# Attention by token: probabilities as the stationary operand of the value products

## What is computed

```python
q = l2norm((h @ Wq.T) by heads) * q_scale      # k likewise; v plain
attn = softmax(einsum('bhid,bhjd->bhij', q, k) * DH ** -0.5)
out = einsum('bhij,bhjd->bhid', attn, v)       # (b, h, 512, 64)
x = x + ga * (out.transpose(0, 2, 1, 3).reshape(b, n, 1024) @ Wo.T + bo)
```

## Time and profile before

| | |
|---|---|
| median of three runs | 1406.56 us |
| the profiled execution: its own time | 1406.78 us |
| the profiled execution: its span | 1405.0 us |
| TensorE matmul busy over the span | 1262.1 us (90%) |
| VectorE busy | 1107.3 us (79%) |
| ScalarE busy | 952.9 us (68%) |
| GpSimd busy | 858.0 us (61%) |

### The profile page before, as it was taken

How to read it: one execution, slowest core, us unless ns; L and a number is a source line. 1 busy time by engine, 2 the same in 40 slices (tenths; PEclk the granted TensorE clock), 3 DMA queues, 4 the chain that set the end, 5 groups by cost and what they waited for, 6 DMA issues and landing times. The chain is left out here.

```text
span 1405.0 us, 31811 instructions
## 1 busy us (share of the span) xinstructions
PE 1262.1 (90%) x9674; PEld 828.6 (59%) x9674; DVE 1107.3 (79%) x1995; ACT 952.9 (68%) x2014; POOL 858.0 (61%) x1659
## 2 busy tenths in 40 slices
PE   4899999989999999999899999999994477899997
PEld 4555565656555565556566555666552355677775
DVE  3778878878878887788788788877873996788887
ACT  3677677767666776677677766777762565777776
POOL 2577666766666776666667667676754664444443
PEclk8899999999999999999999999999998699999999
DMA  5000000000000000000000000000002000535341
GB/s 131 2 2 1 2 1 2 2 4 2 1 4 2 2 2 4 2 2 2 4 1 2 3 2 2 2 1 2 2 1 75 1 0 9 131 86 104 89 89 38
DMA packets 53202, 28.60 MB, mean 20 GB/s; under 512 B 8720, under 2 KB 51224, under 8 KB 53016
## 3 DMA queue, kind: packets, MB, share of 16 engines
q1 hardware_dynamic: 51832, 25.99, 7.7%
q10 hardware_dynamic: 1184, 0.40, 0.1%
HBM read 24.16 MB, written 2.23 MB: 19 GB/s over the span
## 5 line engine op out<-in xcount | busy, mean ns | idle before, releaser
L697 ACT ACTIVATE probs<-bank,neg_max 128x512 f32<-128x512 f32 x512 | 347.5, 684 | 280.3 <-DVE neg_max L815 259.5
L815 DVE TENSOR_REDUCE neg_max<-bank 128x1 f32<-128x512 f32 x512 | 329.3, 685 | 165.4 <-PE bank L516 162.0
L556 PE MATMUL bank<-probsT,qkv 128*64 128x512 f32 x1024 | 280.7, 628 | 0.9 <-DVE oT L832 0.9
L516 PE MATMUL bank<-operands 64*128 64x512 f32 x1536 | 255.9, 439 | 0.9 <-DVE operands L810 0.5
L993 POOL TENSOR_TENSOR inv_wide<-inv_sum,consts 128x512 f32<-128x512 f32 x64 | 66.5, 1039 | 237.7 <-DVE inv_sum L826 237.7
L532 PEld LDWEIGHTS T<-ident,probs 64*128 64x128 f32 x4096 | 173.6, 142 | 40.3 <-issue 10.2
L532 PE MATMUL T<-ident,probs 64*128 64x64 f32 x4096 | 173.6, 226 | 1.5 <-issue 0.7
L486 PEld LDWEIGHTS bank<-operands,hT_h 128*128 128x128 f32 x254 | 48.2, 190 | 213.0 <-issue 209.4
L516 PEld LDWEIGHTS bank<-operands 64*128 64x128 f32 x1536 | 128.4, 190 | 63.5 <-issue 44.2
L1627 POOL TENSOR_TENSOR hid_l<-gated,hid_h 128x512 fp32r<-128x512 f32 x64 | 89.4, 1397 | 123.3 <-ACT hid_h L1544 123.3
L977 POOL TENSOR_TENSOR sq<-qkv 128x256 f32<-128x256 f32 x252 | 150.9, 615 | 11.9 <-ACT qkv L676 9.7
(11 more groups left out here) (235 smaller groups left out, 2399.7 us busy)
## 6 DMA issues: line engine op xcount, KB each, us to landing
probsT<-gate_scratch SPq DMA_DIRECT2D x64, 256.0 KB, 4.9
out<-x_all SPq DMA_DIRECT2D x8, 256.0 KB, 2.3
probsT<-in_L_ffn_fc_w SPq DMA_DIRECT2D x1, 1024.0 KB, 9.4
raw<-in_L_attn_Wq SPq DMA_DIRECT2D x1, 512.0 KB, 4.4
raw<-in_L_attn_Wk SPq DMA_DIRECT2D x1, 512.0 KB, 7.3
raw<-in_L_attn_Wv SPq DMA_DIRECT2D x1, 512.0 KB, 8.6
raw_o<-in_L_attn_Wo SPq DMA_DIRECT2D x1, 512.0 KB, 8.7
probsT<-in_L_ffn_sh_w SPq DMA_DIRECT2D x2, 256.0 KB, 2.7
```

The source lines that it names most:

```text
L516: last = nc.tensor.matmul(s_bank(hp, 2 * pair + head)[:], own[rows, q, toks], own[rows, k], start=((q, k) == (QH, KH)), stop=(q == QL))
L556: last = nc.tensor.matmul(O_BANK[rows, :], qkv[:, hp % 4, j, cols], probsT[:, hp % 2, head, j], start=(j == 0), stop=(j == NT - 1), skip_g ...
L697: nc.scalar.activation(probs[:, i % 4], s_bank(hp, i)[:], ACT.Exp, bias=neg_max[:, i:i + 1], accum_out=row_sum[:, hp % 2, i:i + 1]).then_i ...
L815: nc.vector.reduce_max(neg_max[:, i:i + 1], s_bank(hp, i)[:], AX.X, negate=True).then_inc(max_done, 1)
```

## The change

The value products are turned round: for one tile t of 128 query tokens and one head, the transposed probabilities (128 keys x 128 tokens) are stationary and the values (64 columns) move, four key blocks summed. The result has tokens on the partitions, where the inverse sums already are. Hence:

- TensorE: 32 products of 64 columns per unit for 8 of 512 columns. They stand ahead of the scores of a step instead of behind the transposes of the probabilities, and tile t needs only copy t. `inverse_rows` goes, `transpose_out` (four transposes of the normalised result, in step 1, two units later) takes its place in the shared bank.
- ScalarE: copies three of four transposed tiles; `copy_inverse` goes, `high_o` (same shape, out of the shared bank) takes its place.
- VectorE: copies one of four tiles; `normalise` moves to step 0 and multiplies with a broadcast of the inverse sums; `low_o` is new, in step 1 after the two `row_max`, and reads the shared bank; `ln_rows` uses another instruction; `split_h1` goes to GpSimd.
- GpSimd: `widen` and `split_o` go, `split_h1` comes.

```diff
-                        before, count = ((t_act, 0), (t_dve, 1), (t_act, 1), (t_dve, 2))[pair]
-                        after(pe, before, 2 * u + count)
+                        before, value = ((t_act, 3 * u), (t_dve, u + 1), (t_act, 3 * u + 1), (t_act, 3 * u + 2))[pair]
+                        after(pe, before, value)
...
+                    def transpose_out(w, *free):
+                        pe.wait_ge(o_done, w + 1)
...
+                            last = nc.tensor.transpose(XT_BANK[:, t * P:(t + 1) * P], o_tok[:, t], ident[:])
+                        last.then_inc(ot_ready, 1)
...
-                            last = nc.tensor.matmul(O_BANK[rows, :], qkv[:, hp % 4, j, cols],
-                                                    probsT[:, hp % 2, head, j], start=(j == 0), stop=(j == NT - 1),
+                            at = (2 * t + head) * DH
+                            cols = slice(2 * P + head * DH, 2 * P + (head + 1) * DH)
+                            for j in range(NT):
+                                last = nc.tensor.matmul(O_BANK[:, at:at + DH], by_pair[:, t, head, j], qkv[:, hp % 4, j, cols],
+                                                        start=(j == 0), stop=(j == NT - 1))
...
-                            if pair == 1 and earlier >= 1:
-                                inverse_rows(u - 1, side)
-                                side = (r_copied, u)
+                            if pair == 1 and earlier >= 2:
+                                transpose_out(u - 2, side)
+                                side = (ol_done, u - 1)
                             if main and pair == 2 and with_next(b, hp, 1):
                                 transpose_q(u + 1, hp + 1, side)
                             if main and pair == 3 and with_next(b, hp, 1):
                                 transpose_k(u + 1, hp + 1)
+                            if earlier >= 1:
+                                weigh_values(u - 1, hp - 1, pair)
                             if main:
                                 scores(u, hp, pair)
                             if pair < 2 and earlier >= 1:
                                 transpose_probs(u - 1, pair + 2)
                             if pair >= 2 and main:
                                 transpose_probs(u, pair - 2)
-                            if pair < 2 and earlier >= 2:
-                                weigh_values(u - 2, hp - 2, pair + 2)
-                            if pair >= 2 and earlier >= 1:
-                                weigh_values(u - 1, hp - 1, pair - 2)
...
+                    def high_o(w, hp):
+                        act.wait_ge(ot_ready, w + 1)
+                        nc.scalar.activation(oT_h[:, hp % HP], XT_BANK[:], ACT.Copy).then_inc(oh_done, 1)
...
+                    def low_o(w, hp):
+                        dve.wait_ge(oh_done, w + 1)
+                        nc.vector.tensor_tensor(oT_l[:, hp % HP], XT_BANK[:], oT_h[:, hp % HP].bitcast(F32),
+                                                ALU.subtract).then_inc(ol_done, 1)
...
                                 row_max(u, hp, 2 * pair + 1)
+                            if pair == 1 and earlier >= 2:
+                                low_o(u - 2, hp - 2)
...
-                    last = nc.vector.tensor_scalar(h_ln[:, t], tile_of(b, t), mean_var[:, t, 0:1], rstd[:, t:t + 1],
-                                                   ALU.subtract, ALU.mult)
+                    last = nc.vector.scalar_tensor_tensor(out=h_ln[:, t], in0=tile_of(b, t), scalar=mean_var[:, t, 0:1],
+                                                          in1=rstd[:, t:t + 1].to_broadcast([P, C]), op0=ALU.subtract,
+                                                          op1=ALU.mult)
```

More of the change, by code:

```diff
@@ L542, in inverse_rows, with weigh_values @@
                         for t in range(NT):
[L543 to L552, removed]
+                            last = nc.tensor.transpose(XT_BANK[:, t * P:(t + 1) * P], o_tok[:, t], ident[:])
+                        last.then_inc(ot_ready, 1)
+                    def weigh_values(w, hp, t):
+                        copied, value = ((t_dve, w + 1), (t_act, 3 * w + 1), (t_act, 3 * w + 2), (t_act, 3 * w + 3))[t]
+                        pe.wait_ge(copied, value)
+                        if t == 0:
+                            after(pe, o_done, w)
                         for head in range(2):
[L554 removed]
+                            at = (2 * t + head) * DH
                             cols = slice(2 * P + head * DH, 2 * P + (head + 1) * DH)
[L556 to L559 removed]
+                            for j in range(NT):
+                                last = nc.tensor.matmul(O_BANK[:, at:at + DH], by_pair[:, t, head, j], qkv[:, hp % 4, j, cols],
+                                                        start=(j == 0), stop=(j == NT - 1))
+                        last.then_inc(av_done, 1)
                     def project_out(b, k, *free):
@@ L662, in _ @@
                     slot(B, 0, main=False)
-                    for j in (2, 3):
-                        weigh_values(HP * B - 1, HP - 1, j)
-                    project_out(LAST, 3, (r_copied, HP * B), (y_more, 3 * LAST + 2))
+                    transpose_out(HP * B - 1, (ol_done, HP * B - 1))
+                    project_out(LAST, 3, (y_more, 3 * LAST + 2))
                     transpose_y(LAST)
@@ L744, in slot @@
                                     modulate2(b - 1)
-                            if pair == 1 and earlier >= 1:
-                                copy_inverse(u - 1, hp - 1)
+                            if pair == 1 and earlier >= 2:
+                                high_o(u - 2, hp - 2)
                             if main and pair == 2 and with_next(b, hp, 1):
@@ L753, in slot @@
                                 exponentials(u, hp, 2 * pair + 1)
-                            if pair == 1 and earlier >= 1:
-                                copy_transposed(u - 1, hp - 1, 3)
+                            if pair < 2 and earlier >= 1:
+                                copy_transposed(u - 1, hp - 1, pair + 2)
                             if pair == 3 and main:
@@ L779, in _ @@
                     slot(B, 0, main=False)
+                    high_o(HP * B - 1, HP - 1)
                     for q in range(H2_EARLY, B - 1):
@@ L838, in take_mod @@
                         last.then_inc(done, 1)
[L840 to L847, removed]
                     def add_y(b, k):
@@ L915, in slot @@
                         for pair in range(NT):
-                            if pair == 2 and earlier >= 2:
+                            if pair == 0 and earlier >= 2:
                                 normalise(u - 2, hp - 2)
@@ L927, in slot @@
                                 row_max(u, hp, 2 * pair)
+                                if pair == 0 and hp == YT_HP and not is_const(b, 0):
+                                    dve.wait_ge(x1_done, b)
                                 row_max(u, hp, 2 * pair + 1)
+                            if pair == 1 and earlier >= 2:
+                                low_o(u - 2, hp - 2)
                             if main and pair == 2 and with_next(b, hp, 1):
@@ L932, in slot @@
                                 low_k(u + 1, hp + 1)
-                            if main and pair == 0 and hp == YT_HP and not is_const(b, 0):
-                                dve.wait_ge(x1_done, b)
-                            if pair == 0 and earlier >= 1:
-                                copy_transposed(u - 1, hp - 1, 2)
                             if pair == 2 and main:
@@ L946, in _ @@
                     take_mod(mod1, (CA, SA), 0, mod1_done, (h1_done, 0))
-                    for t in range(NT):
-                        split_h1(0, t)
                     sum_squares(0)
@@ L957, in _ @@
                     normalise(HP * B - 1, HP - 1)
+                    low_o(HP * B - 1, HP - 1)
                     add_y(LAST, 3)
@@ L1014, in slot @@
                             inverse_std(pool, h1_nth(b + 1))
-                        if main and with_next(b, hp, 2):
-                            square_projection(u + 2, hp + 2, 0)
-                        if earlier >= 2:
-                            split_o(u - 2, hp - 2)
-                        if main and with_next(b, hp, 2):
-                            for t in range(1, NT):
+                        for t in range(NT):
+                            if main and with_next(b, hp, 2):
                                 square_projection(u + 2, hp + 2, t)
+                            if main and hp == HP - 3 and not is_const(b, LAST):
+                                split_h1(b + 1, t)
                     def batch(b):
@@ L1025, in batch @@
                             slot(b, hp)
+                    for t in range(NT):
+                        split_h1(0, t)
                     normalise_qk(0, 0)
```

74 lines of the change are left out of this document (27 added, 47 removed).

## The result

The changed kernel takes 1756.22 us (median of 4 runs, 1752.23 to 1759.18) for 1409.73 of the kernel before beside it: a ratio of 1.2458, 95% interval 1.2402 to 1.2513. The forecast was 1733 with a range of 1600 to 1950; the difference forecast was 327 us, measured 346.5. The profiled execution, the slowest of the four, has a span of 1757.5 us, 352.5 more than before.

What follows compares the result with a forecast made beforehand. TensorE, full in every step, bounds the kernel: plus 49.0 us a batch for products and waits, minus 7.6, gives 41.4, times 8 = 331, 327 after the edges; span 1405 + 327 = 1732, forecast 1733 us, range 1600 to 1950.

Steps and rivals of the forecast that it cites:

- What bounds the kernel: Attention stretch: TensorE has no room, busy 967 of 1020 us, so a microsecond more in a step lengthens the whole.
- The products: Value products on TensorE: loads 0.111 us apart, 1.77 us a step for 1.01, plus 3.08 a unit.
- third rival: Value products: loads not hidden, load and product one behind the other, 217 us more, 1950 us; chance 0.07.
- Their place: Value products ahead of the scores: three new TensorE waits for VectorE's low halves, about 1.2 us each a unit.
- E: The end of a step's scores on TensorE, from which the forecast counts its waits in us.
- first rival: The new TensorE waits are covered after all and only the products cost: 1546 us; chance 0.08.
- The norm stalls go: Two norms a batch: shorter VectorE rows fit into the longer step, so TensorE's stalls vanish, minus 7.2 us a batch.
- The batch: Time from one batch's gate to the next: 170 us, where it was 128.6.
- The ends: First and last batch lack some waits at their edges: 327 us more in all for 331.
- second rival: The clock falls behind the new waits, 1.3 us of slow work at each of 192: 1983 us; chance 0.10.
- Costed at nothing: ScalarE's extra copy, VectorE's and GpSimd's changed work, unmoved DMA and the tail's chain: about no cost.

Runs made afterwards that it cites:

- e1_behind: The changed kernel with each step's value products moved back behind the transposes of the probabilities; 1541.91 us, ratio 1.0955 to the kernel before.
- e4_wide: The changed kernel with value products of 128 columns moving for 64, the number of loads unchanged, another output; 1754.23 us.
- e7_gpsimd_load: The changed kernel with four unused 128x512 multiplications on GpSimd ahead of the last squares of the norm slots; 1799.41 us.
- e6_old_norm: The changed kernel with the norm rows made by the old VectorE instruction; 1761.63 us, ratio 1.2458 to the kernel before.

## Why the prediction was right, point by point

- **What bounds the kernel** (TensorE, full in every step): right. With half of the value products left out the time is 230 us shorter, to 1% the sum of their loads.
- **The products**, 0.111 us a load and a step of 1.77 for 1.01: right. Measured 0.111; the next scores follow in 4.33 us in e1_behind for 3.55 to 3.56 before, 0.78 more for 0.77. The third rival, loads not hidden, is refuted by e4_wide. By the strict sentence of the Trainium skill ("TensorE: Matmul & The Clock Gate", The mechanism) loads and products of the same rows would not overlap, which is that rival; this case's traces don't agree: in e4_wide 128 columns, about 0.107 us, pass in the 0.111 us of a load that uses all rows.
- **Their place**, three waits to E + 2.04, 2.10 and 2.04: right. Beside the scores at 535.62 and 540.95 above, the changed kernel has these:

```profile
525.02 0.97 PE L515 MATMUL bank<-operands 64*128 64x512 f32 x6
531.34 0.97 PE L515 MATMUL bank<-operands 64*128 64x512 f32 x6
546.32 0.97 PE L515 MATMUL bank<-operands 64*128 64x512 f32 x6
```

  That makes steps of 4.28, 5.33, 5.37 and 6.32 (with an output projection), forecast as 4.33, 5.37, 5.43 and 6.37. Of the 347 us, undoing the place alone gives back 214. The first rival (the waits are covered) came out where it was priced, 1546, as soon as the cover was put back: 1542.
- **The norm stalls go, minus 7.2 a batch**: they went, but by luck: the step that gave the reason failed. I put it down to the two-tensor instruction. It is GpSimd's instructions beside them that slow VectorE's 128x128 rows in SBUF, from 0.34 to between 0.65 and 1.4 us, and the change took those instructions away from there. The durations of the earlier trace rows were the same thing: in the kernel before, that instruction takes 0.60 us beside a square (at 509.51, the square from 509.35 to 509.97) and 1.08 beside the spreading of the inverse sums (at 517.95); I had read the median as the price of the instruction. The four rows took 1.4 to 1.5 us, inside my 1.2 to 2.4. Had GpSimd stayed busy there, they would not have fitted into the long step: e7_gpsimd_load has the stalls back, and takes 43 us more.
- **The batch**: 170.0 forecast, 170.1 measured. That it is so close is luck too, as small errors cancel: each step was some 0.05 us shorter, 1.6 a batch, and between the first and the last gate the clock fell to 1.2 GHz six times, 24 us in all. Three of these falls came behind a router that itself follows one of the new waits, three behind a loop end with 2.3 us of idle. If half of that time is lost, that is an estimate of 1.7 a batch. A stretch of the changed kernel with the longest fall (the clock is the 0.83) follows; in the kernel before the clock fell behind a norm stall.

```profile
300.00:320.00 20.00, 17.39 (x144) 0.83 0.00 1
```

- **The ends, minus 4 in my sum**: mis-sized. The gates account for 290.6 of the 352.5 us of span; the two ends together have 61.9 for the 41.4 - 4 = 37.4 of the sum. The first gate is 37.6 later, about six units at 5.2 with the start, and from the last gate to the end there are 399.4 us for 375.1, 24.3 more. Two units explain 10 of these. I had called the tail even; it has four groups of value products that nothing lies beside, and in this execution they ran at the lower clock. The last two groups of the changed kernel, of e4_wide and of e6_old_norm:

```profile
1410.60 7.09 PE L555 MATMUL bank<-qkv,probsT 128*128 128x64 f32 x32
```

```profile
1410.30 3.84 PE L555 MATMUL bank<-qkv,probsT 128*128 128x128 f32 x32
```

```profile
1408.56 3.79 PE L554 MATMUL bank<-qkv,probsT 128*128 128x64 f32 x32
```

  7.09 us at 1.2 GHz for 3.84 and 3.79 at 2.4. From the last gate to the end e4_wide takes 390.1 us and e6_old_norm 390.2, both 9 less than the changed kernel, and their first gates came at 160.0 and 162.1 for 167.3. The value products of e6_old_norm are those of the changed kernel, so the same products ran here at the lower level in one execution and at the higher in another; what decides it stays open. Some 5 us of the tail stay open. This is the second rival, the clock, in a small form. It did not follow the three waits of a unit, as I had feared.
- **Costed at nothing**: right. In the attention stretch TensorE waited once for ScalarE's exponentials (0.9 us), once for GpSimd (1.3 us), and for VectorE only in the low halves and `normalise`, which stand in the sum.

## What to carry to other kernels

Before turning a product round, count its weight loads: with few columns moving, each 128-column f32 load cost 0.11 us here at 2.4 GHz, with 8, 64 or 128 columns moving behind it. And before moving a block of work ahead, look for what it hid: a bank's reader on another engine, issued behind something that waits for your own last result, needs a time that does not shrink (here 2.04 us behind the scores), and the block may have been all that covered it. Do not read a price off the median of an instruction that is slow only in places: compare what the neighbour engine does there before replacing the instruction, and when you hold the neighbour back, hold back only what nobody waits for.

## What the runs showed of the hardware

- A 128x128 f32 instruction of VectorE in SBUF, the old one or the new, took 0.34 us alone. Beside a large instruction of GpSimd it lasted about as long as that one: 0.65 to 0.70 beside a square (0.61), 1.08 and 1.43 beside the two halves of the split (1.04 and 1.27), 1.12 beside a 128x512 multiplication (1.08). I had expected the instruction's kind to matter.
- Weight loads of 128 columns in f32, one after the other, start 0.111 us apart at 2.4 GHz, with 64 or with 128 columns moving, and 7.09 / 32 = 0.22 us at 1.2 GHz.
- The same kernel's tail can run at either clock level: the last 32 products took 7.09 us at 1.2 GHz in the changed kernel, and 3.79 at 2.4 in e6_old_norm, which differs from it in one VectorE instruction.
